# The blocks of a graph-attention layer: one PSUM bank per half of the features, and a fixed engine for each half

## The reference

```python
s1 = einsum('bkf,ef->bke', h, W1);  s2 = einsum('bkf,ef->bke', h, W2)     # e: 256 features; W = adj
pre = s1[:, :, None, :] + s2[:, None, :, :] + b_lin                       # 256 x 256 x 256 per batch
e = einsum('bije,e->bij', where(pre >= 0, pre, 0.2 * pre), a) + adj
out = sigmoid(einsum('bij,bjf->bif', softmax(e, axis=2), h))
```

```python
z = sigmoid(av @ w3.T + b3 + u3);  r = sigmoid(av @ w4.T + b4 + u3)
hv = tanh(av @ w5.T + b5 + (r * h @ u5.T + bu5));  h = (1 - z) * h + z * hv     # 5 times
```

## Time and profile before

| | us |
|---|---|
| median of 3 runs | 5788.99 |
| lowest, highest | 5787.91, 5806.22 |
| profiled execution | 5805.18 |
| span in its profile | 5803.3 |

### The profile page before, as it was taken

How to read it: one execution, slowest core, us unless ns; L and a number is a source line. 1 busy time by engine, 2 the same in 40 slices (tenths; PEclk the granted TensorE clock), 3 DMA queues, 4 the chain that set the end, 5 groups by cost and what they waited for, 6 DMA issues and landing times.

```text
span 5803.3 us, 127250 instructions
## 1 busy us (share of the span) xinstructions
PE 5645.7 (97%) x40844; PEld 2229.1 (38%) x40844; DVE 4974.7 (86%) x9389; ACT 5268.6 (91%) x12857; POOL 4982.9 (86%) x10246
## 2 busy tenths in 40 slices
PE   8999999999999999999999999999999999999997
PEld 2333333333334333333333333333433333333334
DVE  8888988888888888888898888888888888888883
ACT  8999999999999999999998999999999999999993
POOL 8988988889888888888898888988888888889880
PEclk9999999999999999999999999999999999999999
DMA  0000000000000000000000000000000000000000
GB/s 14 5 3 7 7 8 4 6 7 7 8 6 3 7 7 8 6 3 7 7 7 8 2 7 7 7 8 6 3 7 7 8 6 3 7 7 7 7 5 6
DMA packets 44539, 37.19 MB, mean 6 GB/s; under 512 B 4736, under 2 KB 39552, under 8 KB 43648
## 3 DMA queue, kind: packets, MB, share of 16 engines
q1 hardware_dynamic: 43648, 26.56, 1.5%
HBM read 9.77 MB, written 8.39 MB: 3 GB/s over the span
## 4 chain that ended last, share of the span: by engine, by line
PE 83%; ACT 9%; issue 3%; DVE 3%; POOL 2%; DMA 0%; SPq 0%; POOLq 0%; DVEq 0%; ACTq 0%
PE S L995 52%; PE R L943 13%; ACT ring L798 6%; PE W L943 5%; PE S L943 4%; PE R L1132 2%; PE PA L943 2%; POOL ring L491 1%; PE R L1140 1%; DVE ring L601 1%; PE PB L943 1%; ACT h L840 1%; PE S L987 1%; PE PB L1020 1%; ACT prob L822 0%
## 5 line engine op out<-in xcount | busy, mean ns | idle before, releaser
L491 POOL TENSOR_SCALAR ring<-W,U 128x256 f32<-128x256 f32 x9536 | 4673.8, 509 | 212.8 <-PE S L995 169.3
L798 ACT ACTIVATE ring<-W,U_minus 128x256 f32<-128x256 f32 x10336 | 4239.7, 505 | 0.1
L995 PE MATMUL S<-ring,a_window 128*32 128x512 f32 x32768 | 3732.2, 596 | 52.7 <-DVE ring L601 18.7
L601 DVE TENSOR_TENSOR ring<-U,W 128x512 f32<-128x512 f32 (+1 forms) x3808 | 3187.1, 861 | 3.8 <-PE S L995 3.7
L995 PEld LDWEIGHTS S<-ring,a_window 128*32 128x32 f32 x32768 | 1028.8, 110 | 2464.8 <-issue 2361.9
L596 DVE TENSOR_TENSOR ring<-U,W 128x256 f32<-128x256 f32 x2592 | 1040.4, 407 | 0.0
L462 POOL TENSOR_TENSOR minus_mean<-mv,minus_one 128x4 f32<-128x4 f32 (+1 forms) x160 | 31.5, 197 | 506.8 <-DVE mv L661 469.7
L943 PE MATMUL R<-mT,W 128*128 128x512 f32 (+1 forms) x640 | 332.8, 602 | 2.1 <-ACT mT L902 2.1
L943 PE MATMUL R<-AT,h 128*128 128x256 f32 x1260 | 308.3, 388 | 2.7 <-ACT h L914 2.1
L734 DVE SCALAR_TENSOR_TENSOR rh<-tr,h3T 128x512 f32<-128x512 f32 (+1 forms) x165 | 146.3, 887 | 188.1 <-ACT tr L905 187.8
L738 DVE TENSOR_TENSOR diff<-cand,h3T 128x512 f32<-128x512 f32 (+1 forms) x165 | 192.6, 1167 | 110.3 <-ACT cand L911 110.3
(11 more groups left out here) (173 smaller groups left out, 4070.4 us busy)
## 6 DMA issues: line engine op xcount, KB each, us to landing
X<-in_x SPq DMA_DIRECT2D x64, 128.0 KB, 2.1
X_held<-X SPq DMA_DIRECT2D x32, 256.0 KB, 3.0
out<-OUT SPq DMA_DIRECT2D x64, 128.0 KB, 1.9
raw<-in_L_gnn_w_w SPq DMA_DIRECT2D x3, 128.0 KB, 2.3
A<-in_adj SPq DMA_DIRECT2D x1, 256.0 KB, 2.8
Wn<-in_L_gnn_Wn SPq DMA_DIRECT2D x1, 128.0 KB, 2.5
Wm<-in_L_gnn_Wm SPq DMA_DIRECT2D x1, 128.0 KB, 2.6
rawu<-in_L_gnn_u_w SPq DMA_DIRECT2D x2, 64.0 KB, 2.2
```

What stands on the lines that cost most here:

```text
L491: last = gp.tensor_scalar(ring[:, place, g, half * N:(half + 1) * N], W[:, y, c], LARGEST, U[:, y, c, i:i + 1], ALU.min, ALU.max)
L601: piece = dve.tensor_tensor(ring[:, place, g:g + groups].rearrange("p g (h j) -> p g h j", h=NB), u.unsqueeze(3).to_broadcast([P, groups, ...
L798: last = act.activation(ring[:, place, g, half * N:(half + 1) * N], W[:, y, c], ACT.Relu, bias=U_minus[:, y, c, i:i + 1])
L995: last = pe.matmul(S[y][g * ROWS:(g + 1) * ROWS, :], a_window[:, c, ROWS - 1 - row:2 * ROWS - 1 - row], ring[:, place, g], start=False, st ...
```

## The change

Each chunk of W gets a bank of its own, `W_bank[y][c]`, which holds W of the chunk in its left half and U before the bias in its right half. PA and PB are gone: the bank `W_bank[y][1]` of the batch that isn't being worked on takes over their jobs (`side[y]`). VectorE makes blocks only of chunk 0 (even lots), reading W from the first bank; ScalarE only of chunk 1 (odd lots), reading W from the second bank rather than from SBUF; GpSimd fills up what is missing in either. TensorE waits for two engines at most per lot. U_minus is made by ScalarE for chunk 1 only, with minus_b0 as its bias, in a step of its own between the two copies.

The planner now goes by pairs of lots and has a cost for each lot that GpSimd takes part in (POOL_START). VectorE's pieces of a pair may be held back in both positions of the pair.

```diff
-VECTOR_BLOCK, VECTOR_START, SCALAR_BLOCK, POOL_BLOCK = 2.67, 0.69, 3.57, 4.5
+VECTOR_BLOCK, VECTOR_START, SCALAR_BLOCK, POOL_BLOCK, POOL_START = 2.67, 0.69, 3.57, 4.5, 2.2
...
-        put(vector, PRE[h], half, stats=5.5, evacuate=0.6)
-        put(scalar, PRE[h], half, norm=5, copy=2.6, evacuate=12)
+        put(vector, PRE[h], half, stats=5.5)
+        put(scalar, PRE[h], half, norm=7.7, copy=3.6, evacuate=18)
...
-        d, g, a = min(((d, BLOCKS - d - a, a) for d in range(1, BLOCKS) for a in range(1, BLOCKS - d)), key=ends)
-        shares.append((d, g, a))
+        d, a = min(((d, a) for d in range(1, BLOCKS + 1) for a in range(1, BLOCKS + 1)), key=lambda da: sorted(costs(*da), reverse=True))
+        shares += [(d, BLOCKS - d, 0), (0, BLOCKS - a, a)]
...
-        for at in (POST[h]["score"], POST[h]["transpose"], PRE[h]["stats"]):
+        for at in (POST[h]["transpose"], PRE[h]["stats"]):
...
-    for _ in range(SPARE_BLOCKS[t]):
+    for _ in range(sum(SPARE_BLOCKS[t:t + EC])):
...
-        W_bank = [bank("W0"), bank("W1")]
-        PA, PB = bank("PA"), bank("PB")
+        W_bank = [[bank(f"W{y}{c}") for c in range(EC)] for y in range(2)]
+        side = [W_bank[y][1] for y in range(2)]
...
-            def finish_lot():
-                while lot["done"] < len(lot["pieces"]):
+            def finish_lot(t):
+                held = SPARE_BLOCKS[t + 1] if t % EC == 0 else 0
+                while lot["done"] < len(lot["pieces"]) - held:
                     one_piece()
...
-                if p == PRE[1 - y]["evacuate"]:
-                    dve.wait_ge(u_ready, value)
-                    dve.tensor_scalar(U_minus[:, y], U[:, y], -1.0, None, ALU.mult).then_inc(u_minus_ready, 1)
...
-                    last = act.activation(ring[:, place, g, half * N:(half + 1) * N], W[:, y, c], ACT.Relu,
-                                          bias=U_minus[:, y, c, i:i + 1])
+                    last = act.activation(ring[:, place, g, half * N:(half + 1) * N], W_bank[y][1][:, 0:N], ACT.Relu,
+                                          bias=U_minus[:, y, i:i + 1])
...
-                    for c in range(EC):
-                        last = act.activation(U[:, y, c], PB[:, c * N:(c + 1) * N], ACT.Identity, bias=b0_col[:, c:c + 1])
-                    last.then_inc(u_ready, 1)
-                    act.activation(W[:, y], W_bank[y][:].rearrange("p (c n) -> p c n", c=EC), ACT.Copy).then_inc(w_ready, 1)
+                    for c, bank_ in enumerate(W_bank[y]):
+                        act.activation(U[:, y, c], bank_[:, N:2 * N], ACT.Identity, bias=b0_col[:, c:c + 1])
+                        if c == 1:
+                            act.activation(U_minus[:, y], bank_[:, N:2 * N], ACT.Identity, bias=minus_b0[:, c:c + 1], scale=-1.0)
+                        act.activation(W[:, y, c], bank_[:, 0:N], ACT.Copy).then_inc(uw_ready[c], 1)
...
-                pe.wait_ge(by_dve[place], turn.at(ROUNDS, rnd + 1))
-                pe.wait_ge(by_act[place], turn.at(ROUNDS, rnd + 1))
-                pe.wait_ge(by_pool[place], turn.at(ROUNDS, rnd + 1))
+                pe.wait_ge((by_dve, by_act)[c][place], turn.at(ROUNDS, rnd + 1))
+                if SHARES[t][1]:
+                    before, per_turn = pool_lots(t)
+                    pe.wait_ge(by_pool[place], turn.at(per_turn, before + 1))
```

More of the change, by code:

```diff
@@ L115, in share_blocks, with costs, pool_lots @@
     shares, v, s, q = [], 0.0, 0.0, 0.0
-    for t in range(LOTS):
-        def ends(share):
-            d, g, a = share
-            return sorted((v + VECTOR_START * (1 + d % 2) + d * VECTOR_BLOCK, q + g * POOL_BLOCK, s + a * SCALAR_BLOCK), reverse=True)
-        d, g, a = min(((d, BLOCKS - d - a, a) for d in range(1, BLOCKS) for a in range(1, BLOCKS - d)), key=ends)
-        shares.append((d, g, a))
-        v += VECTOR_START * (1 + d % 2) + d * VECTOR_BLOCK + vector[t]
-        q += g * POOL_BLOCK + pool[t]
-        s += a * SCALAR_BLOCK + scalar[t]
+    for t in range(0, LOTS, EC):
+        def costs(d, a):
+            by_pool = [BLOCKS - d, BLOCKS - a]
+            return (v + VECTOR_START * (1 + d % 2) + d * VECTOR_BLOCK,
+                    q + sum(g * POOL_BLOCK + (POOL_START if g else 0) for g in by_pool), s + a * SCALAR_BLOCK)
+        d, a = min(((d, a) for d in range(1, BLOCKS + 1) for a in range(1, BLOCKS + 1)), key=lambda da: sorted(costs(*da), reverse=True))
+        v, q, s = costs(d, a)
+        shares += [(d, BLOCKS - d, 0), (0, BLOCKS - a, a)]
+        v += sum(vector[t:t + EC])
+        q += sum(pool[t:t + EC])
+        s += sum(scalar[t:t + EC])
     return shares
 SHARES = share_blocks()
+def pool_lots(t):
+    has = [SHARES[n][1] > 0 for n in range(t % RING, LOTS, RING)]
+    return sum(has[:t // RING]), sum(has)
 def spare_blocks():
@@ L481, in blocks @@
                 d, count, _ = SHARES[t]
-                if p == 0:
-                    gp.wait_ge(u_ready, turn.at(2, y + 1))
-                    gp.wait_ge(w_ready, turn.at(2, y + 1))
+                if row == 0:
+                    gp.wait_ge(uw_ready[c], turn.at(2, y + 1))
+                if not count:
+                    return
                 need(gp, freed[place], turn.at(ROUNDS, rnd))
@@ L764, in body @@
                     y, p = divmod(t, LOTS_B)
-                    if turn.has_main:
+                    if turn.has_main and t % EC == 0:
                         start_lot(turn, t)
@@ L831, in post @@
                     for r in range(NB):
-                        last = act.activation(tanh0[:, r], PA[:, r * P:(r + 1) * P], ACT.Tanh, scale=half_inv[:, r:r + 1])
+                        last = act.activation(tanh0[:, r], side[y][:, r * P:(r + 1) * P], ACT.Tanh, scale=half_inv[:, r:r + 1])
                     last.then_inc(tanh0_ready, 1)
@@ L1009, in pre @@
                         pe.wait_ge(*bank_read)
-                    for j, bank_ in enumerate((PB, W_bank[y])):
+                    for j in range(2):
                         for c in range(EC):
-                            last = mm(bank_[:, c * N:(c + 1) * N], (AT[:, 0], AT_minus)[j][:, c * P:(c + 1) * P], H0T[:, y])
+                            last = mm(W_bank[y][c][:, (1 - j) * N:(2 - j) * N], (AT[:, 0], AT_minus)[j][:, c * P:(c + 1) * P], H0T[:, y])
                     last.then_inc(uw_psum, 1)
@@ L1025, in post @@
                         for j in range(NB):
[L1026 removed]
+                            last = mm(side[y][:, i * P:(i + 1) * P], probT[:, j, i * P:(i + 1) * P], H0[:, y, j], j == 0, j == NB - 1)
                     last.then_inc(attn_psum, 1)
@@ L1162, in body @@
                     if turn.has_main and (y == 0 or turn.pre_next):
-                        pre(p, 1 - y, turn.at(2, y + 2), (x3_ready if y else recvT_ready, turn.at(1, 0)) if turn.has_l12 else None)
+                        pre(p, 1 - y, turn.at(2, y + 2), (x3_ready if y else recvT_ready, turn.at(1, 0)) if turn.has_l12 else None,
+                            (src_ready, turn.at(1, 0)) if turn.has_l12 and y == 0 else None)
                     if turn.has_l12:
```

77 lines of the change are left out of this document (40 added, 37 removed).

## The result

The changed kernel takes 5880.18 us (median of 4 runs, 5873.78 to 5984.04) against 5789.36 for the kernel before (4 runs): ratio 1.015, 95% interval 1.0127 to 1.0172. I had predicted 5825, a ratio of 1.0062. The direction and the range held, the size didn't: 91 us were lost, not 36.

A forecast was written before the change was run, and what follows sets the result against it. TensorE, busy 97%, was taken to bound full turns, the block makers turn 0. On the profiled scale 5805.18 - 17 (turns 0 and 1) + 54 (30 full turns at +1.8) = 5842, as a median 5825 us; 8-in-10 range 5760 to 5885.

The forecast's parts named there:

- the sum of the waits: TensorE's waits for VectorE at the five layer 3 states, lots 28, 50, 72, 94, 116: 2.6 us per full turn.
- Step 0: Layer 3's state before lot 28: six ScalarE blocks, `diff` 0.80 us; TensorE waits 0.3 us a turn (0 to 0.5).
- The chain formula: Layer 3, from `tz` through blocks, `cand`, `diff`, `gated` and pieces to the lot: 3.10 + 0.36 n + `diff` us.
- Rival C: Holds of `diff` grow to 3.08 us in two more steps: 120 us more, median about 5945; chance 0.06.
- Step 2: Layer 3's state before lot 72: six ScalarE blocks, `diff` near its median 1.009 us; TensorE waits 0.6 us a turn.
- Steps 1, 3 and 4: Layer 3's states before lots 50, 94 and 116: TensorE waits 0.9, 0.7 and 0.1 us a turn.
- The semaphore: One semaphore fewer per lot on TensorE: costed at nothing, since lots already follow one another at 0.858 us.
- Turns 0 and 1: First two turns, where block makers set or share the time: -10 and -7 us, together -17 (-8 to -25).
- The bigger lots of GpSimd: Up to seven blocks or 3.2 us, covered by the ring's eight places: costed at nothing; otherwise up to 1 us a turn.
- Rival A: VectorE and ScalarE run ahead, five waits together below 0.8 us: median 5748, up to 5770; chance 0.26.
- Rivals B and D: B: waits about half, 1.3 us, median 5787, chance 0.17. D: ScalarE no quicker from PSUM, median 5855, chance 0.06.

The follow-up runs named there:

- the changed kernel run again: The changed kernel, unaltered, run again against the kernel before, for another profile and ratio: 5896.54 us, ratio 1.0196.
- The stops of 2.8 us: Best version (few blocks before candidate, nothing held back at layer 3 states, POOL_START 0) plus 12 SyncE round trips before lot 106: ratio 1.0057 to the kernel before.
- stops of 5.8 us: Same best version, with 24 semaphore round trips to SyncE holding TensorE before lot 106 in 30 turns: ratio 1.0267 to the kernel before.

## Why the prediction was wrong in size

The step that failed is the sum of the waits, in two of its five terms, steps 0 and 2: together 0.9 us a turn in the forecast, 3.26 in the profile. Its formula held within 0.2 us; what it had wrong is how long VectorE's operation is held up, and where.

**Step 0, mis-sized: 0.3, measured 1.43.** The chain formula was right, one of its terms wasn't. VectorE's timeline at the first wait above, and GpSimd's:

```profile
3101.93 3.53 DVE L748 TENSOR_TENSOR diff<-cand,h3T 128x512 f32<-128x512 f32 x1 [1.16 <-ACT cand L921]
3105.37 0.68 DVE L614 TENSOR_TENSOR ring<-U,W 128x512 f32<-128x512 f32 x1
3105.97 0.79 DVE L752 SCALAR_TENSOR_TENSOR gated<-tz,diff 128x512 f32<-128x512 f32 x1
3106.68 0.67 DVE L614 TENSOR_TENSOR ring<-U,W 128x512 f32<-128x512 f32 x1
```

```profile
3096.57 10.98 POOL L503 TENSOR_SCALAR ring<-W,U 128x256 f32<-128x256 f32 x22
```

`diff` lasted 3.53 us where I had put 0.80. In step 0 it was over 2 us in 14 of the 30 turns (11 in the changed kernel run again), and never in the other steps. In those 14 turns TensorE waited 2.4 to 2.9 us before lot 28, in the other 16 about 0.5, the high end that I had given. Before, it was over 2 us in 24 of 30 turns of step 2 and in no other step. I saw one such row at step 2 and set it against the median over all steps, which has four times as many of the others; the median of step 2 alone was 3.08. The hold wasn't rare, it belonged to one place, and the change moved it. Rival C, which had such holds come in two more steps, was half right on the mechanism: they came in one, and left another.

What goes with a hold of `diff` is GpSimd at work. In the changed kernel run again there are 145 full-sized `diff` in turns 2 to 30. In the 42 during which GpSimd was at work for less than half of the time it took 0.68 to 0.81 us. Of the other 103, 11 took 3.08 to 3.52 us and the rest at most 1.08, so no hold was seen without GpSimd at work, and most `diff` with it were not held. The run of 22 blocks above goes on beyond the end of `diff`; some 2.8 us of hold are about six of its blocks, which start 0.45 us apart. The block of GpSimd that was under way when a hold ended took 1.0 us rather than 0.5, in all 11 cases. The Trainium skill, "SBUF — State Buffer", section "Who interferes with whom", has the loser blocked until the first instruction has finished. That the two contend, the traces bear out; that one block is the longest hold, by which I had named 1.1 us, they don't. What picks the block behind which VectorE gets through, they don't show.

**Step 2, mis-sized: 0.6, measured 1.83.** Here I had borrowed the room of 5.91 us from step 3. TensorE's group from 3171.05 puts lot 72 at 3176.20, and ScalarE's rows are:

```profile
3170.72 0.57 ACT L885 ACTIVATE h2T<-W 128x512 f32<-128x512 f32 x1
3171.20 0.67 ACT L918 ACTIVATE tz<-R,bias 128x512 f32<-128x512 f32 x1
3171.77 2.29 ACT L807 ACTIVATE ring<-W,U_minus 128x256 f32<-128x256 f32 x6
3173.90 0.73 ACT L921 ACTIVATE cand<-R,bias 128x512 f32<-128x512 f32 x1
```

The room was 5.0 us. `tz` doesn't come when TensorE gives it, but behind the softmax of the batch before, which waits for VectorE's maximum. So it is in 11 of the 30 turns, with a wait of 1.25 us. In the other 19 `rh` lasted 2.3 to 2.8 us and stood before the maximum on VectorE, the room was 3.8 us, and the wait 2.06 to 2.36. In such a turn of the changed kernel run again, where ScalarE waited 2.25 us for the maximum:

```profile
2969.08 2.77 DVE L744 SCALAR_TENSOR_TENSOR rh<-tr,h3T 128x512 f32<-128x512 f32 x1 [2.72 <-ACT tr L915]
...
2979.52 0.69 DVE L748 TENSOR_TENSOR diff<-cand,h3T 128x512 f32<-128x512 f32 x1 [2.38 <-ACT cand L921]
```

The same kind of hold, one operation earlier. The length from `tz` to the lot's end is as forecast: 3.10 + 6 x 0.36 + 1.01 = 6.27 by the formula, 6.46 to TensorE's start. The size of the chain was right and the room it had to fit in was not looked up.

**Steps 1, 3 and 4: right within 0.3.** 0.65, 0.42 and 0.30 against 0.9, 0.7 and 0.1. In step 1 `diff` was at its short form (0.69 at 3140.00), the case that gave my low end of 0.6.

**What a wait costs, left out.** I took 1 us of wait for 1 us of time. The stops of 2.8 us cost 1.5 us per us. In the changed kernel run again the matmuls of the lots are busy 84 us longer than without kept pieces, on top of 130 us of added waits. That is more than the waits themselves were mis-sized by, (4.3 - 2.6) x 30 = 51.

**The semaphore, costed at nothing: a gain of 0.7 to 1.5 us a turn.** "Lots already follow one another at 0.858" was true of the rows that I looked at and not of the first eight lots behind the loop edge, of which I had said that the change doesn't touch it. So the most to be won was not 0.8 us a turn; without the kept pieces a turn takes 176 us rather than 178.65.

**Turns 0 and 1: -5.6 us rather than -17.** Turn 0 took 139.29 (forecast 136), with VectorE the busiest as forecast, but at 136.90 us rather than 134.6, and 2.4 us not busy. Turn 1 took 151.65 (forecast 144): nobody is over 143 us busy, but TensorE waits for GpSimd, 2.59 us at one lot. The bigger lots of GpSimd, costed at nothing under cover of the ring, are not covered in turn 1; its waits for GpSimd are 4.9 us there.

**Right as forecast.** ScalarE's blocks 0.36 apart; VectorE's pieces of six and eight blocks at 1.74 and 2.28 us, on the same slope; no wait before lot 73; `cand` late behind six blocks. Rival A (waits below 0.8) is what the kernel would have been without its kept pieces: 0.9921 against the 0.993 that I gave it. Rivals B and D fall.

In the sum, on the scale of the kernel run again: turns 0 and 1 -5.6 rather than -17; waits 4.3 rather than 2.6 a turn; the lower clock behind them; less a gain at the loop edge. That leaves +4 us a turn by the medians, (114 + 6) / 30, where I had +1.8. How these shares stand in the timed executions, 75 us shorter than the profiled one, no profile shows.

## What to carry to other kernels

Where total work falls and chains grow, look for each chain's own due time and its own durations, step by step; a median over steps hides an operation that is slow at one place in every turn. Price a stop of TensorE by more than its length when it is as long as those that the half clock followed here, 2 us and more. Before keeping work back to fill gaps between dependent steps, ask who waits for that work: here it was the next lot that TensorE wanted, and dropping it gained 2.7% and won back a change that looked lost.

## What the runs showed of the hardware

- A stop of TensorE of 2.8 us was followed by 3.4 us at a granted clock of 0.5 in 17 of 29 cases, and these cost 1.6 to 1.7 us each; stops of 5.8 us cost 2.6 us beyond themselves in the mean, and all 29 had such a stretch.
- Satisfied waits of TensorE, three rather than one or two per lot, left the lots at 0.858 us within a turn, and cost 1.7 us within the first eight lots behind the edge of the hardware loop.
- A round trip of semaphores between TensorE and SyncE took 0.24 us, and sixteen of them before lot 104 cost nothing that shows.
- The VectorE operation `diff`, 128x512 with two SBUF inputs, took 0.68 to 0.81 us with GpSimd mostly idle. With GpSimd at work it took up to 3.5 us in the changed kernel, the length of about six GpSimd blocks more, and an operation of 0.45 us took 9.33 where GpSimd's blocks followed one another without a pause.
- ScalarE makes a 128x256 block in 0.36 us from PSUM and in 0.40 from SBUF.
